# Rotary attention: scores from three short-fp32 products of high and low parts

## The reference, cut to what matters

```python
q = jnp.einsum('bsd,hd->bsh', x, wq)
k = jnp.einsum('bsd,hd->bsh', x, wk)
v = jnp.einsum('bsd,hd->bsh', x, wv)
...
q = apply_rope(q)
k = apply_rope(k)
scale = float(np.sqrt(hd))
w = jax.nn.softmax(jnp.einsum('bqh,bkh->bqk', q, k) / scale, axis=-1)
out = jnp.einsum('bqk,bkh->bqh', w, v)
return jnp.einsum('bsh,dh->bsd', out, wo)
```

## Time and profile before

| | us |
|---|---|
| median of 3 runs | 4145.25 |
| lowest to highest | 4142.39 to 4164.42 |
| the profiled execution | 4151.7 |
| its span | 4150.0 |
| PE busy | 3930.1 (95%) |
| DVE busy | 2798.7 (67%) |
| ACT busy | 2639.6 (64%) |
| POOL busy | 1556.3 (38%) |
| the rotary stage, from its layer norm to its last matmul | about 2393 to 2830 |

### The profile page before, as it was taken

How to read it: one execution, slowest core, us unless ns; L and a number is a source line. 1 busy time by engine, 2 the same in 40 slices (tenths; PEclk the granted TensorE clock), 3 DMA queues, 4 the chain that set the end, 5 groups by cost and what they waited for, 6 DMA issues and landing times. The chain is left out here.

```text
span 4150.0 us, 65963 instructions
## 1 busy us (share of the span) xinstructions
PE 3930.1 (95%) x23476; PEld 2360.4 (57%) x23476; DVE 2798.7 (67%) x5635; ACT 2639.6 (64%) x3262; POOL 1556.3 (38%) x1303
## 2 busy tenths in 40 slices
PE   7999999999969999999999989997999999999999
PEld 4555545555457787887878855554444444444444
DVE  7978888888578878788787555444545555554553
ACT  2666666666765545455454334444888888888888
POOL 3222222222334445344353221111555455555545
PEclk8999999999979999999999999998999999999999
DMA  7543544444132232322323210005676766667674
GB/s 180 127 105 85 114 100 101 107 92 116 43 119 61 83 101 62 109 75 81 103 61 106 63 35 1 1 1 121 143 163 145 165 152 154 154 146 160 150 160 100
DMA packets 205762, 430.00 MB, mean 104 GB/s; under 512 B 47584, under 2 KB 72560, under 8 KB 189056
## 3 DMA queue, kind: packets, MB, share of 16 engines
q1 hardware_dynamic: 193360, 411.56, 41.0%
q0 software_dynamic: 4160, 6.35, 0.7%
q10 hardware_dynamic: 7920, 7.87, 0.6%
HBM read 338.59 MB, written 87.03 MB: 103 GB/s over the span
## 5 line engine op out<-in xcount | busy, mean ns | idle before, releaser
L2254 ACT ACTIVATE gelu_out<-hidden,b_col 128x1024 f32<-128x1024 f32 x1024 | 1054.5, 1117 | 182.9 <-PE hidden L2177 177.5
L2237 POOL TENSOR_TENSOR combined<-combined,gated 128x512 f32<-128x512 f32 x480 | 621.3, 1294 | 648.9 <-DVE gated L2354 473.2
L715 DVE TENSOR_REDUCE maxima<-front_and_scoresT 128x1 f32<-128x512 f32 (+3 forms) x1280 | 725.9, 630 | 79.5 <-PE front_and_scoresT L517 49.8
L615 ACT ACTIVATE probsT<-front_and_scoresT 128x1024 f32<-128x1024 f32 (+3 forms) x768 | 596.6, 811 | 263.7 <-PE front_and_scoresT L550 258.4
L1179 POOL TENSOR_TENSOR pair_sums<-sims 128x1024 f32<-128x1024 f32 x256 | 482.9, 1902 | 662.6 <-DVEq L1311 412.3
L2354 DVE SCALAR_TENSOR_TENSOR gated<-out_bank,b_col,gates_spread 128x512 f32<-128x512 f32 x480 | 360.3, 751 | 512.3 <-PE out_bank L2185 483.6
L2177 PE MATMUL hidden<-slice_stack,w_stack 128*128 128x512 f32 x2048 | 623.2, 428 | 37.9 <-ACT gelu_out L2254 37.8
L1107 PE MATMUL dense<-xnT,dense_weights 128*128 128x512 f32 x2304 | 537.3, 395 | 12.5 <-ACT silu_down L1213 8.6
L2177 PEld LDWEIGHTS hidden<-slice_stack,w_stack 128*128 128x128 f32 x2048 | 354.9, 190 | 327.0 <-ACT gelu_out L2254 249.6
L2185 PE MATMUL out_bank<-gelu_out,w_sb 128*32 128x512 f32 x4096 | 517.1, 607 | 3.2 <-DVE combined L2354 3.0
L1107 PEld LDWEIGHTS dense<-xnT,dense_weights 128*128 128x128 f32 x2304 | 434.9, 189 | 112.9 <-ACT silu_down L1213 9.2
(11 more groups left out here) (202 smaller groups left out, 5069.2 us busy)
## 6 DMA issues: line engine op xcount, KB each, us to landing
gates_spread<-gate_scratch SPq DMA_DIRECT2D x512, 256.0 KB, 5.4
dense_weights<-dense_scratch SPq DMA_DIRECT2D x384, 256.0 KB, 2.8
stack_scratch<-split_parts SPq DMA_DIRECT2D x192, 256.0 KB, 3.1
slice_stack<-slice_scratch SPq DMA_DIRECT2D x128, 256.0 KB, 8.1
q_stack<-stack_scratch SPq DMA_DIRECT2D x64, 384.0 KB, 6.2
k_stack<-stack_scratch SPq DMA_DIRECT2D x64, 384.0 KB, 9.2
slice_scratch<-slice_parts SPq DMA_DIRECT2D x32, 512.0 KB, 5.6
out_x<-x_tiles ACTq DMA_DIRECT2D x15, 512.0 KB, 2.9
```

The costliest lines, as they stand in the source:

```text
L615: nc.scalar.activation(PT[:, i % NPT, 2 * pr:2 * pr + 2, at:BANK], R[:, low:high + 1:high - low, at:BANK], ACT.Exp, scale=SCALE).then_inc( ...
L715: nc.vector.tensor_reduce(dst, bank(k)[:, 0:parts * w].rearrange("p (a k) -> p a k", a=parts), AX.X, ALU.max)\
L2237: nc.gpsimd.tensor_tensor(CM[:, par, hc, :], CM[:, par, hc, :], Y[:, u % 2, :], ALU.add)\
L2254: nc.scalar.activation(GH[:, k % GHB, :, :], HP[k % HPB][:, :, :], ACT.Gelu, bias=b1c[:, n % E:n % E + 1])\
```

## The change

The turned queries and keys are no longer kept as fp32 but as two F32R tensors, a high part (the value rounded to F32R) and a low part (what is left). The score of 512 keys is then the sum of three F32R products, high by high, high by low and low by high, in place of one fp32 product. To make the parts, POOL adds into `RC` in place; ACT copies `RC` to the high part (`high_part`); POOL subtracts the high part from `RC` into the low part. The next key or query block on POOL starts after that subtraction. ACT does `high_part` after `exps(n)` and before its copies of the step; ahead of the first step swap and `high_part` alternate.

The second tensor takes the room of `W1R`: W1 is now loaded in two halves into the buffer of the raw attention weights, the first once these are turned, the second once the first has been rounded. DVE rounds at n = 20 and n = 30.

```diff
-    SPLIT_AT = 20
+    SPLIT_AT = 20, 30
...
+    PARTS = ((0, 0), (0, 1), (1, 0))
...
-        QK = sb("turned_qk", [HD, 2, 2, T])
+        QK = sb("turned_qk", [HD, 2, 2, 2, T], F32R)
...
-        W1R = sb("w1_raw", [P, later.E, later.I])
+        W1R = RAW[:, :, :].rearrange("p a d -> p (a d)").rearrange("p (e i) -> p e i", i=later.I)
...
         def _(sp):
+            sp.wait_ge(w_ready, 4)
             later.load(sp, W1R)
+            later.load_half(sp, W1R, 1)
...
                     pe.wait_ge(rope_ready, r_count("k", b, q))
-                    mm = nc.tensor.matmul(SC[n % 2][:, q * BANK:(q + 1) * BANK], QK[:, 0, b % 2, t * P:(t + 1) * P],
-                                          QK[:, 1, b % 2, q * BANK:(q + 1) * BANK], start=True, stop=True)
+                    for j, (of_q, of_k) in enumerate(PARTS):
+                        mm = nc.tensor.matmul(SC[n % 2][:, q * BANK:(q + 1) * BANK],
+                                              QK[:, of_q, 0, b % 2, t * P:(t + 1) * P],
+                                              QK[:, of_k, 1, b % 2, q * BANK:(q + 1) * BANK], start=(j == 0), stop=(j == 2))
                 mm.then_inc(scores_done, 1)
...
-                nc.gpsimd.tensor_tensor(QK[:, SIDES.index(kind), b % 2, tok], RC[:, n % 2, :], SW[:, n % 2, :], ALU.add)\
+                nc.gpsimd.tensor_tensor(RC[:, n % 2, :], RC[:, n % 2, :], SW[:, n % 2, :], ALU.add).then_inc(rope_summed, 1)
+                pool.wait_ge(rope_high, n)
+                nc.gpsimd.tensor_tensor(QK[:, 1, SIDES.index(kind), b % 2, tok], RC[:, n % 2, :],
+                                        QK[:, 0, SIDES.index(kind), b % 2, tok].bitcast(F32), ALU.subtract)\
                   .then_inc(rope_ready, 1)
...
+            def high_part(kind, b, i):
+                n = r_count(kind, b, i)
+                act.wait_ge(rope_summed, n)
+                nc.scalar.activation(QK[:, 0, SIDES.index(kind), b % 2, i * BANK:(i + 1) * BANK], RC[:, n % 2, :], ACT.Copy)\
+                   .then_inc(rope_high, 1)
...
-            for kind, i in FRONT_FIRST:
-                if kind in SIDES:
-                    swap(kind, 0, i)
+            for k, i in R_ORDER:
+                swap(k, 0, i)
+                high_part(k, 0, i)
             for n in range(STEPS):
                 for unit in front_units(n):
                     if unit[0] in SIDES:
                         swap(*unit)
                 if n < NT:
                     exps(n)
+                for unit in front_units(n):
+                    if unit[0] in SIDES:
+                        high_part(*unit)
                 if n in PV_AT:
                     keep_product(PV_AT[n])
...
-                if n == SPLIT_AT:
-                    later.split(dve, W1R)
+                if n in SPLIT_AT:
+                    later.split(dve, W1R, SPLIT_AT.index(n))
...
-    def split(self, dve, raw):
+        self.load_half(sp, raw, 0)
+
+    def load_half(self, sp, raw, k):
+        wait(sp, self.half_split, k)
+        experts = slice(k * self.E // 2, (k + 1) * self.E // 2)
+        for j in range(self.G):
+            sp.dma_start(raw[self.HD * j:self.HD * (j + 1), :, :], self.arrays[3][experts].rearrange("e d i -> d e i"),
+                         allow_slow_non_contiguous=True).then_inc(self.half_in[k], 16)
...
+        part = self.w1s[:, k * self.E // 2:(k + 1) * self.E // 2, :]
+        self.nc.vector.tensor_copy(part, raw[:, :, :]).then_inc(self.rounded, 1)
+        dve.wait_ge(self.rounded, k + 1)
+        self.nc.vector.tensor_tensor(part[low], raw[low, :, :], part[low].bitcast(F32), ALU.subtract)\
+            .then_inc(self.half_split, 1)
```

More of the change, by code:

```diff
@@ L1561, in rotary_attention @@
         sin_ready = sem("sin1_ready")
+        rope_summed = sem("rope1_summed")
+        rope_high = sem("rope1_high")
         rope_ready = sem("rope1_ready")
@@ L1921, in __init__ @@
         self.weights_in = ctx.enter_context(nc.semaphore("weights2_in"))
+        self.half_in = [ctx.enter_context(nc.semaphore(f"w1_half{k}_in")) for k in range(2)]
+        self.half_split = ctx.enter_context(nc.semaphore("w1_half_split"))
         self.rounded = ctx.enter_context(nc.semaphore("w1_rounded"))
@@ L1936, in load @@
             row = slice(self.HD * j, self.HD * (j + 1))
-            moves += [(raw[row, :, :], W1.rearrange("e d i -> d e i")), (self.b2c[row, :], b2.rearrange("e o -> o e")),
-                      (self.embd[row, j, :], emb)]
+            moves += [(self.b2c[row, :], b2.rearrange("e o -> o e")), (self.embd[row, j, :], emb)]
         self.all_in = 16 * len(moves)
@@ L1942, in load, with split @@
             sp.dma_start(dst, src, allow_slow_non_contiguous=True).then_inc(self.weights_in, 16)
-    def split(self, dve, raw):
-        low = slice(2 * self.HD, 4 * self.HD)
[L1947 to L1950, removed]
+        self.load_half(sp, raw, 0)
[5 more added lines that the diff above has]
+                         allow_slow_non_contiguous=True).then_inc(self.half_in[k], 16)
+    def split(self, dve, raw, k):
+        low = slice(2 * self.HD, 4 * self.HD)
+        if k == 0:
+            dve.wait_ge(self.weights_in, self.all_in)
+        dve.wait_ge(self.half_in[k], 16 * self.G)
+        part = self.w1s[:, k * self.E // 2:(k + 1) * self.E // 2, :]
[3 more added lines that the diff above has]
+            .then_inc(self.half_split, 1)
 def mixture_ffn(nc, X, STATS, MEAN, RS, B, weights, out, ident):
```

## The result

| | before | after |
|---|---|---|
| median, us | 4143.86 (4 runs) | 4225.85 (4 runs) |
| ratio to before | 1 | 1.0194 (95% interval 1.0173 to 1.0215) |
| profiled span, us | 4150.0 | 4226.3 |
| rotary stage, first weight load to first expert product, us | 463.2 | 545.8 |
| four tiles in mid-stage, us | 25.97 | about 31.5 |

The forecast was 4216 us, 70.75 more than the median then known; measured are 82 more. The change works as meant on TensorE and loses more on what it put into ACT's queue. The whole difference lies in the rotary stage, which is 82.6 us longer.

The account below looks back on a forecast made before the run. TensorE was taken to bound the rotary stage. Scores -21.9, stalls +70, opening +6, tail +1.5 and clock +15 sum to +71 us: 4222 us for the profiled execution, 4216 us as a median, range 4187 to 4242.

Parts of the forecast that it names:

- The scores: Score products on TensorE: 0.229 us per F32R product, 0.34 us less a tile, 21.9 us less over 64 tiles.
- four passes: Alternative estimate for the scores: true fp32 makes four array passes, so three would save a quarter of 110 us, 27 us.
- The stall: Steps making two key or query blocks: TensorE waits for ACT's copies 14 times, 5.0 us each, 70 us.
- Point 5: TensorE's transposes of tile n's probabilities need a bank freed by ACT's delayed copy: wait from 2619.27 to 2624.3, 5.0 us.
- The opening: Start of the rotary stage: swaps and high parts alternate on ACT, so the first scores' second half comes 6.0 us later.
- The tail: Last batch, without front units: gains 8 x 0.34 us less some 1.5 us, as transposes and last value products wait for ACT.
- The clock: Lower TensorE clock expected behind most of the 14 gaps: 15 us in all, bounds 0 and 24.
- I take 1.1: Time charged per clock drop, in us, from 1.7 of lost work with a part hidden; 15 us in all.
- The small edits: Later W1 loads, DVE's split in two halves, the cosines' wait: zero to 2 us, taken as 0.
- rivals that ended faster: ACT's wait doesn't reach TensorE: 4129 us, or 4123 with the opening hidden; chance 0.05 of over 0.5% faster.
- rival without clock loss: Stalls on TensorE as forecast, but clock kept or its loss inside the gap: +56 us, 4201 us; chance 0.12.
- dear product: Score products cost 0.265 us each, gaining 8 us instead of 22: 4230 us, 4239 with whole clock term; chance 0.10.

Follow-up runs that it names:

- e8: Changed kernel with high parts copied by POOL, x blocks normalised on DVE two steps earlier, second W1 split at n = 28: 4133.6 us, 0.9968 of before.
- e3: Changed kernel plus 20 F32R products on TensorE ahead of the transposes that wait for ACT, in 14 steps: 4201.4 us, 1.0115 of before.
- e5: Changed kernel with q's high part one step later in ACT's queue, behind the next tile's exponentials: 4162.7 us, 1.0045 of before.
- e4: Changed kernel with the high parts copied by POOL between its sum and subtraction, none on ACT: 4170.7 us, 1.0053 of before.

## Why the prediction was right

**What bounds the stage** was read rightly: TensorE, with no slack for a wait.

**The scores** held. In e8, where TensorE waits for nothing that it did not wait for before, four tiles are 1.33 us shorter, 0.33 a tile; 0.34 was worked out from the 0.229 of the earlier trace rows. With 1.72 us a tile before, that makes 0.231 us a product, and 21 us in all. The estimate of 27 us by the four passes is 6 us too high.

**The stall** held in place, number and size: 14, each by the order of the queue. Point 5 had 5.0 us. The gaps are 4.7 (5.5 beside the second split), and four tiles in e3, at full clock, are 29.75 against 24.64 in e8, so a stall costs 5.1 us with the small waits around it. 14 x 5.1 = 71.5, forecast 70.

**The opening** held: TensorE's two gaps there are together 5.2 us longer (below, its timeline, against the earlier trace rows: 2.27 and 1.44), forecast 6. The second half of the first scores starts 32.1 us into the stage instead of 25.9, 6.3 later. Up to the first output product after is 11.9 us longer than before; less one stall (5.1) and its drop of the clock (1.9), and plus the gain of seven tiles (2.3), that is 7.2; the same sum gives 6.2 in e3.

```profile
2413.54 1.65 PE L1677 MATMUL scores<-turned_qk 128*128 128x512 f32 x3 [5.98 <-POOL turned_qk L1744]
...
2418.12 1.65 PE L1677 MATMUL scores<-turned_qk 128*128 128x512 f32 x3 [2.94 <-POOL turned_qk L1744]
```

**The tail**: forecast was that 1.5 us of the last batch's gain are lost. From the 14th output group on, after is 1.6 us shorter where the five tiles left there should give 1.7, and the four tiles before them gain 1.0 and not 1.3 in e8, where no stall hides it. So 0.5 is lost.

**The clock** is the term that was mis-sized: 23.9 us measured by e3 against 15. The step that failed is "Each such drop in these rows is worth 1.7 us", carried over to all 14. The rows had two short drops, one in another stage and one in the opening; ten of the 14 here lose 3.4 us. The next step, "I take 1.1", on the ground that "Some of it falls into the gap itself or on other waits", was right in kind: 41 us of clock were lost and 23.9 reached the time, and the short drops cost 1.2 to 1.4 each, close to 1.1. That the measured term lies so near the upper bound of 24, which was 14 short drops with nothing hidden, is chance, since in the trace the drops are longer and partly hidden. Why some drops are twice as long as others stays open.

With what was measured, the sum is -21.3 (scores) + 71.5 (stalls) + 23.9 (clock) + 7.2 (opening) + 0.5 (tail) + 0.8 (second split) = 82.6 us, and the stage is 82.6 longer. This shows that nothing is left over; it is no check of each term, since opening and tail are what remains of their stretches once the others are taken off. The forecast was 70.6, and 8.9 of the 12 us between them are the clock.

**The small edits** were costed at nothing. The second split lengthens its own four tiles by 0.8 us in after (32.46 against some 31.6), since it slows POOL's subtraction beside it to 2.12 us. The rivals that ended faster fell with the first trace; e5 shows that the place in ACT's queue was 71 of the 82.6 us, and left the kernel slower than before all the same. The rival without clock loss, 4201 us, is what e3 measures (4201.4) once the clock is kept up. That POOL's load slows DVE was in none of my cases. It hardly mattered here, where TensorE waits anyway, but it decided e4. Two slips on the way cost nothing: the upper bound, dear product with the whole clock term, is 4239 by the prediction's own sums and not 4242, and the 5 of 40 us for POOL are one window, where 8 of 40 is the mean from the first output product on.

## What to carry to other kernels

An instruction that waits for another engine costs what stands behind it in its own queue, not its own time: follow the queue to the next thing that the bounding engine needs. Price a new gap on TensorE twice, once for its length and once for the slow clock behind it. Read the second price from drops behind gaps of that kind, and from more than one, since their length differs by a factor of two here; then follow the slow stretch to see which waits it swallows. Before work is moved to an idle GpSimd, look which DVE instructions will run beside it, and whether they can be moved apart.

## What the runs showed of the hardware

- A DVE normalisation of 128x256 fp32 from SBUF to SBUF takes 0.40 us alone and up to 1.43 beside GpSimd; in e4, the 39 that lay beside GpSimd for over nine tenths of their time took 1.10 us in the mean and the 7 that lay free 0.41. Not all of the 39 were slow: twelve, the first of their four, took 0.40, and the other 27 took 1.41 in the mean. GpSimd's own tensor operations beside them stayed at 1.27 to 1.40 us. Beside the split's subtraction on DVE, which reads two tensors, it was GpSimd's subtraction that went from 1.27 to 2.12 us. The Trainium skill, GPSIMD Engine Reference, Specifications, says that the SBUF interfaces are shared with VectorE, with contention from instructions in a 2-port mode or with two SBUF inputs. These runs agree for two inputs (the split); in which mode the normalisation ran no trace shows. They also show that it is the DVE instruction that can lose, by a factor of over three.
- 280 more TensorE products made a kernel 0.6% faster by the medians (4201.4 against 4225.9 us), 0.8% by the ratios to before, since they kept the clock up through waits.
- Every one of the 14 gaps of 4.7 us or more was followed by the lower clock. Twelve gaps of 1.6 us in e5 were not: but for one drop, behind a wait of 1.9 us, its clock is 1.00 there. In e4 a wait of 1.4 us stands in each of 13 periods (and one of 1.9 beside the second split), and six periods have a drop. So the length of the gap alone does not tell.
- The same copy of 128x512 fp32 to F32R in SBUF takes 0.63 us on ACT and 0.61 on GpSimd, while GpSimd's two-input operations of that size take 1.27.
